# A four-layer model on one core: a new hand-written order in the gated delta attention, and three smaller moves

## Chip, core and metric

The kernel runs as one program on one core of a Trainium2 chip. A core has five engines that run side by side, each with its own instruction stream: TensorE (PE, matrix products and transposes), VectorE (DVE), ScalarE (ACT), GpSimd (POOL) and SyncE (SP), which here only issues transfers (DMA). They wait for each other by semaphores. The metric is the device time of the core in microseconds (us), less is better.

## The reference

`x` has 2 sequences of 1024 tokens with 256 channels. Four layers follow each other; in each, attention and feed-forward both read the same normalised `xn`, and both are added to the residual:

```python
xn = layernorm(x)                       # no weights
x = x + attention_l(xn) + feed_forward_l(xn)
```

- Layer 0: gated delta-rule attention with 16 heads (key and value width 128), and a feed-forward whose weights are rounded to -1, 0, 1 (width 704, sigmoid gate).
- Layer 1: causal softmax attention, 16 heads of width 128 over 4 key/value heads, output bias; feed-forward with silu gate, width 1024.
- Layer 2: rotary attention, 16 heads of width 16; 16 experts of which each token takes the best two, squared relu, weights dequantised.
- Layer 3: attention with exponential decay, 32 heads of width 64; 8 experts, best two, and a shared expert of width 704.

The delta rule of layer 0, for one head:

```python
q, k, v = silu(conv4(xn @ Wq.T)), silu(conv4(xn @ Wk.T)), silu(conv4(xn @ Wv.T))
e = k @ Wsv.T - v                       # its l2, l1 and cosine feed two small MLPs
beta, amp = sigmoid(mlp_b(stats)), mlp_a(stats)
g = -exp(A_log) * softplus(k/|k| * amp + dt_bias)     # per channel
for t in tokens:
    S = S * exp(g[t])[:, None]
    delta = (v[t] - kn[t] @ S) * beta[t]
    S = S + outer(kn[t], delta)
    o[t] = qn[t] * 128**-0.5 @ S
out += (rmsnorm(o) * norm_w * sigmoid(xn @ Wg1.T @ Wg2.T + bg2)) @ Wo.T
```

## The kernel before

**Stages.** Nine blocks follow each other: the first layer norm, the delta attention, the first feed-forward, the causal attention, the second feed-forward, the rotary attention, its experts, the decay attention, the last experts. Between two blocks all engines meet at a barrier. The residual `T.x` (tokens on partitions) and the transposed norm `T.xnT` (channels on partitions) stay in SBUF throughout. Each feed-forward normalises the residual for the next layer as its groups of 512 tokens end, the last group at its very end.

**Delta attention.** There are 64 units, one for each head and group of 512 tokens. The recurrence over tokens is turned into matrix work: chunks of 128 tokens, within a chunk a triangular system solved by doubling in seven levels (`LV` = 7, blocks of 1, 2, 4 ... 64 tokens). A new unit starts every seven slots (`SL`), and each operation X of a unit has a fixed slot `X_AT` after its start; `at(g, X_AT)` gives the unit whose X runs in slot g. So each slot holds one level of one unit, one chunk of the unit before, and parts of the preparation of two later units. Every engine has one loop over the slots, and inside it a row of `if` blocks: their order, written by hand, is the order in which that engine works. Nothing is reordered at run time, so an instruction that waits holds up all behind it on its engine.

The names that matter, by engine:

- PE: projections of k, v, q (L296, into the PSUM tensor `fr`), the values turned (L328) and their prediction, statistics `STAT` (L383), `Z` broadcasts, the diagonal `KQ` (L352), transposes of `kF` (`KH`, L376), the gate matmul (`GATE`, L323). Per level: `products(u, lv)` (L305, all pairs of tokens into `lpd`), `transposed` (L310), the x matmul (L396), the yt matmuls (L437, L439 in the last level). Level 0 has transposes of the mask instead (L451). Per chunk k (in the slots of levels 0 to 3 of the next unit): w (L341), dl (L424), o and s (L462 to L467). Then the row sums of squares with one column each (L476) and the output projection Y (L417).
- DVE: three taps of the short convolutions after the first (`convolve`, L680), the mask that copies products into the level matrices `MA` (L691), the polynomial for log(1+x) by Horner steps (L694, in parts `POLY` and `W`), `z` and `kF`, the diagonal (L752, `diag`), `R` (L770), the triangular updates `Tm` (L785, L831) and `TT` in the last level (`TT6`, L789), the halo of the convolution (L817, L819), the state `St` (L842, L844), the gated output `og` (L825).
- ACT: first taps and silu, copies of `TT` (L512), `Xs` (L569), `Dl` (L552), `y` (L560), `khat` (L549), exponentials, the tanh of the gate, squares.
- POOL: per level `scale` (L614 to L616: `kq`, `kF` and the totals of the decays), roots by power, parts of the small MLPs, the adds of `y` to the residual.

In front of the slots PE waits for all constants (6 transfers) and for memsets, computes the first gate projection g1 for all four token groups (L290; the loops issue 8 matmuls, and the trace shows each matmul call as two instructions, here 16), and waits for ACT's copies before the first unit's k projection. DVE and POOL also wait for the constants before their loops.

**Decay attention.** Steps of one unit each; after every `NU3` steps a group of 512 tokens ends with sums, a norm and the output projection. The first group's end also holds the router's logits of the last expert layer for all 16 token tiles (64 matmul instructions of nine columns, L1869), and the best two are picked in one burst of small DVE instructions (`two_best`) shortly after, at step `ROUTE + 3`.

The slots before the change:

```python
K_AT, V_AT, Q_AT, SILU_AT, VT_AT, STAT_AT, SUMS_AT, ROOT_AT = 0, 1, 2, 4, 5, 6, 7, 8
MLP_AT, MLP2_AT, HID_AT, BETA_AT, Z_AT, POLY_AT, W_AT, KQ_AT, LV_AT = 9, 10, 11, 11, 13, 14, 15, 16, 17
GATE_AT, KH_AT, CHUNK_AT, OUT_AT, RMS_AT, Y_AT = 17, 24, 24, 28, 29, 31
```

With seven slots to a unit, level 0 shares its slot with `GATE`, `KH`, the first chunk and Y of older units; level 6 shares its own with `Q_AT` and `KQ_AT`.

## Time and profile before

| | |
|---|---|
| three runs, us | 6602.77, 6605.63, 6611.05 |
| median, us | 6605.63 |
| profiled execution, us | 6588.47, of which the span is 6586.7 |
| busy share of the span | PE 92%, DVE 59%, ACT 41%, POOL 35% |
| mean granted clock of TensorE | 0.96 of full |
| instructions | 99233 |

The profile is one execution, recorded by the hardware profiler. Times in it are us from the start of the span. A line such as L305 is a line of the kernel shown above. In an order of time, a row has its start, its length, engine, line, operation, the tensors written and read, the tile, how many instructions it groups, and in brackets the idle time of the engine ahead of it with what released it. The granted clock is that which the throttle allowed TensorE: 1.0 is 2.4 GHz, 0.5 is 1.2 GHz.

### The profile page before, as it was taken

How to read it: one execution, taken by the hardware profiler on the slowest of the kernel's cores; microseconds unless marked ns; L12 is line 12 of the kernel's file. 1: busy time of each engine (PE TensorE's matmuls, PEld its weight loads, DVE VectorE, ACT ScalarE, POOL GpSimd, SP SyncE). 2: the span in 40 equal slices, each digit the busy share in tenths (PEclk: the TensorE clock that was granted, in tenths of full speed). 3: DMA queues.
4: the chain of work that ended last, by engine and by line, in shares of the span. 5: the costliest groups of instructions: out<-in, count | busy, mean ns of one | idle time of the engine just before them, and what ended most of it. 6: DMA issues, size and time to landing. Idle time of an engine off the chain costs nothing. (4 is left out here: it accounts for less than half of the span.)

```text
span 6586.7 us, 99233 instructions
## 1 busy us (share of the span) xinstructions
PE 6069.7 (92%) x37522; PEld 4392.9 (67%) x37522; DVE 3858.4 (59%) x7222; ACT 2708.2 (41%) x5584; POOL 2308.8 (35%) x2602
## 2 busy tenths in 40 slices
PE   5898989898889898988899999999999989999999
PEld 3777777777777777777477777653334667767665
DVE  5777777777777777775334444337654444444322
ACT  4445454545454444443145555413664122222211
POOL 3666667676666666675000000010000011111100
PEclk8999999999999999999999999998999999999999
DMA  0000000000000000000000000000001011211200
GB/s 29 5 5 5 3 2 5 5 5 5 5 5 1 5 5 5 5 1 1 15 18 14 12 11 12 23 7 1 1 1 52 1 62 62 68 68 68 75 7 7
DMA packets 33925, 112.56 MB, mean 17 GB/s; under 512 B 4272, under 2 KB 9648, under 8 KB 33456
## 3 DMA queue, kind: packets, MB, share of 16 engines
q1 hardware_dynamic: 33456, 106.22, 4.8%
q8 instruction: 305, 5.00, 0.3%
q14 instruction: 164, 1.34, 0.1%
HBM read 104.11 MB, written 2.10 MB: 16 GB/s over the span
## 5 line engine op out<-in xcount | busy, mean ns | idle before, releaser
L614 POOL TENSOR_TENSOR d_kq<-d_kq,d_tot 128x512 f32<-128x512 f32 x448 | 556.6, 1242 | 829.2 <-PE d_lpd L305 823.8
L305 PE MATMUL d_lpd<-d_kq,d_kF 128*128 128x128 f32 x3584 | 550.2, 302 | 110.9 <-POOL d_tot L616 103.3
L680 DVE SCALAR_TENSOR_TENSOR d_qkv<-d_raw,d_wts,d_qkv 128x512 f32<-128x512 f32 x576 | 506.8, 888 | 124.8 <-ACT d_qkv L493 120.0
L305 PEld LDWEIGHTS d_lpd<-d_kq,d_kF 128*128 128x128 f32 x3584 | 491.1, 211 | 133.1 <-POOL d_tot L616 126.5
L691 DVE COPY_PREDICATED d_MA<-d_pairs,d_lpd 128x512 f32<-128x512 int32 x384 | 316.4, 824 | 359.6 <-PE d_lpd L305 356.9
L396 PEld LDWEIGHTS d_xy<-d_Tm,d_MA 128*128 128x128 f32 x3072 | 409.4, 205 | 167.4 <-issue 165.7
L396 PE MATMUL d_xy<-d_Tm,d_MA 128*128 128x64 f32 x3072 | 434.8, 288 | 58.8 <-ACT d_TT L512 57.4
L1744 DVE TENSOR_REDUCE r_nm<-r_ps 128x2 f32<-128x1024 f32 x256 | 307.8, 1223 | 138.6 <-PE r_ps L1563 138.4
L994 POOL TENSOR_TENSOR f1rstd<-f1var,mhalf 128x4 f32<-128x4 f32 x4 | 4.0, 1009 | 1097.1 <-DVE f1var L1019 1097.1
L296 PE MATMUL d_fr<-xnT,d_wts 128*128 128x512 f32 x768 | 380.1, 618 | 0.7 <-ACT d_g1T L487 0.7
L437 PE MATMUL d_xy<-d_Xs,d_TT 128*128 128x64 f32 x2560 | 366.9, 293 | 0.2 <-ACT d_Xs L569 0.2
L1841 PE MATMUL e_pj<-xnT,e_wts 128*128 128x512 f32 x768 | 347.7, 602 | 13.5 <-DMA e_wts<-in_w3all 11.7
L437 PEld LDWEIGHTS d_xy<-d_Xs,d_TT 128*128 128x128 f32 x2560 | 358.4, 216 | 0.4 <-ACT d_Xs L569 0.4
L615 POOL TENSOR_TENSOR d_kF<-d_kF,d_tot 128x256 f32<-128x256 f32 x448 | 352.0, 786 | 0.0
L1664 ACT ACTIVATE r_pT<-r_ps 128x512 f32<-128x512 f32 x512 | 274.9, 598 | 146.3 <-PE r_ps L1571 145.7
L694 DVE SCALAR_TENSOR_TENSOR d_lp<-d_lp,d_ez 128x512 f32<-128x512 f32 x448 | 325.0, 725 | 13.1
L512 ACT ACTIVATE d_TT<-d_xy 128x256 f32<-128x256 f32 x320 | 124.5, 389 | 464.3 <-PE d_xy L310 464.3
L1304 DVE TENSOR_TENSOR c_sc<-c_sc,c_mask 128x128 f32<-128x128 f32 x256 | 76.7, 300 | 397.8 <-PE c_sc L1181 397.8
L1219 PEld LDWEIGHTS c_po<-c_pT,c_vt 128*128 128x128 f32 x2304 | 294.7, 191 | 21.0 <-ACT c_pT L1279 9.3
L1219 PE MATMUL c_po<-c_pT,c_vt 128*128 128x128 f32 x2304 | 301.9, 276 | 0.2
L1563 PE MATMUL r_ps<-r_kT,r_qT 32*128 32x512 f32 x1024 | 292.1, 694 | 2.7 <-DVE r_nm L1744 1.1
L642 POOL TENSOR_TENSOR d_pw<-d_st,d_half 128x20 f32<-128x20 f32 x64 | 257.5, 4024 | 98.6 <-DVE d_sums L706 98.5
(399 smaller groups left out, 13919.4 us busy)
## 6 DMA issues: line engine op xcount, KB each, us to landing
e_wts<-in_w3all SPq DMA_DIRECT2D x64, 897.0 KB, 4.6
d_wts<-in_headw SPq DMA_DIRECT2D x16, 583.5 KB, 3.8
c_wqo<-in_wqo SPq DMA_DIRECT2D x32, 256.0 KB, 2.6
f3ws<-in_f3w SPq DMA_DIRECT2D x17, 384.0 KB, 8.2
f2ws<-in_f2s SPq DMA_DIRECT2D x16, 256.0 KB, 6.6
f2qs<-in_f2q SPq DMA_DIRECT2D x16, 256.0 KB, 6.8
f1ws<-in_f1w SPq DMA_DIRECT2D x8, 384.0 KB, 6.4
f0ws<-in_f0w SPq DMA_DIRECT2D x6, 384.0 KB, 5.4
```

The lines of the kernel that those rows point to most:

```text
L296: last = nc.tensor.matmul(fr[:, bank, :], w_of(u)[:, w0 + kd * P:w0 + (kd + 1) * P], T.xnT[:, kd, tok(u):tok(u) + GRP], start=(kd == 0), s ...
L305: last = nc.tensor.matmul(out[:, :, k], kF[:, u % 2, ch_(k)], moving[:, :, k, :, 1], start=True, stop=True)
L396: last = nc.tensor.matmul(mh(xy[:, j * 64:(j + 1) * 64], h), MA[:, lv, ch_(j)], even(Tm[:, ch_(j)], h), start=True, stop=True)
L437: last = nc.tensor.matmul(xy[:, 256 + j * 64:256 + (j + 1) * 64], TT[:, ul % 2, ch_(j)], Xs[:, j * 64:(j + 1) * 64], start=True, stop=True)
L614: nc.gpsimd.tensor_tensor(v, v, bc(bc(t_l[:, :, 0], 2, h), 1, 2), ALU.mult)
L615: nc.gpsimd.tensor_tensor(f, f, bc(t_l[:, :, 1], 2, h), ALU.mult)
L680: step = nc.vector.scalar_tensor_tensor(qkv[:, u % 3, x], raw[:, u % 2, x, i:i + GRP], tap(u, x, i), qkv[:, u % 3, x], ALU.mult, ALU.add)
L691: nc.vector.copy_predicated(into, bc(mh(pairs[:, lv], h), 1, 2), lpd[:].rearrange("p (x m h) -> p x m h", x=2, h=h)).then_inc(masked, 1)
L694: ch.link(nc.vector.scalar_tensor_tensor(lp[:], lp[:], LOG1P[i], ez[:], ALU.add, ALU.mult))
L1219: last = nc.tensor.matmul(po[:, 0:P], vt[:, n // (4 * QT) % 2, j], pT[:, n % 2, j * P:(j + 1) * P], start=(j == 0), stop=(j == t))
L1744: nc.vector.tensor_reduce(nm[:, t % 2, half, 4 * j + i0:4 * j + i0 + 2], ps[:, row_pair(row - 1):row_pair(row - 1) + 2], AX, ALU.max).then ...
L1841: last = nc.tensor.matmul(pj[:, x % 2, :], w[:, w0 + kd * P:w0 + (kd + 1) * P], T.xnT[:, kd, g * GRP:(g + 1) * GRP], start=(kd == 0), stop ...
```

## The change

**The order in the delta attention** is written anew on all four engines.

- PE, in a slot: k projection, statistics, values, `Z`, `KQ`, w, products(0), the x matmul, Y, dl, `KH`, q projection, products, yt, o and s, the row sums, and for level 0 the transposes and products(1), then the v projection, the gate matmul, and the transposes of the later levels. `KH` moves one slot earlier (`KH_AT` 24 to 23, the slot of level 6). In the level-0 slot Y now precedes dl, o and s, and these precede the transposes and products(1); the gate goes from first to last.
- DVE: the small MLP instructions and the level-0 mask go to the front of the slot; the taps are mostly placed early; the masks precede `og`, the diagonal, `Tm` and `St`; in level 4 Horner steps precede the mask; in level 6 `TT6` and the third tap of v precede the diagonal; `kF` and the halo follow `St`.
- ACT: `khat` and `R` first, the copies of y ahead of `Dl`, then `Xs`, the squares and the evacuations of q and v, last the tanh of the gate, the error squares, `Z`, the exponential of beta and the evacuation of k.
- POOL: roots ahead of the second MLP part; scale ahead of the first `kq` product; the second scaling of level 0 behind the first two adds of y.

**The front.** The first head's weights are the first transfer, ahead of the constants. The g1 projections move to slot 3 (into the PSUM tensors `lpd`, `xy`, `ca`, `co`), with their waits for the constants and memsets; ACT copies them at the start of slot 4, ahead of its silu; PE waits for these copies at slot 17. DVE and POOL wait for the constants at slot 6.

**The norm of the first feed-forward.** It normalises three of its four groups (`norms=NG - 1`). The causal attention does the last: DVE's mean, centring and variance at its start, ACT's square between its first evacuations of keys, POOL's power ahead of the addition of the bias to the residual (which now waits for the norm), PE's eight transposes after the first two score tiles, ACT's two copies into `T.xnT` after the first softmax tile.

**The routing.** The logits come in three portions, at the ends of the first three groups: 8, 4 and 4 token tiles. `ROUTE` goes from `NU3 + 1` to `3 * NU3 + 1`, and `two_best` is cut into four parts that run at steps `ROUTE + 3` to `ROUTE + 6`; the shared gate follows at `ROUTE + 7`.

The core of the diff (the moves within ACT, POOL and DVE are given by some of their lines; "..." stands for lines left out):

```diff
-GATE_AT, KH_AT, CHUNK_AT, OUT_AT, RMS_AT, Y_AT = 17, 24, 24, 28, 29, 31
+GATE_AT, KH_AT, CHUNK_AT, OUT_AT, RMS_AT, Y_AT = 17, 23, 24, 28, 29, 31
...
+        G1_SLOT = 3
...
+                sp.dma_start(wts[:, 0], ins["headw"][0]).then_inc(loaded[0], 16)
...
-                pe.wait_ge(const_loaded, 96)
-                pe.wait_ge(consts_set, 4)
-                for t in range(NG):
-                    for kd in range(KD):
-                        last = nc.tensor.matmul(fr[:, t, :], wg1[:, kd], T.xnT[:, kd, t * GRP:(t + 1) * GRP], start=(kd == 0), stop=(kd == KD - 1))
-                    last.then_inc(g1_mm, 1)
-                pe.wait_ge(g1_copied, NG)
...
+                    if g == G1_SLOT:
+                        pe.wait_ge(const_loaded, 96)
+                        pe.wait_ge(consts_set, 4)
+                        for t, bank in enumerate((lpd, xy, ca, co)):
+                            for kd in range(KD):
+                                last = nc.tensor.matmul(bank[:], wg1[:, kd], T.xnT[:, kd, t * GRP:(t + 1) * GRP], start=(kd == 0), stop=(kd == KD - 1))
+                            last.then_inc(g1_mm, 1)
+                    if g == LV_AT:
+                        pe.wait_ge(g1_copied, NG)
...
+                    if level and lv == 0:
+                        pe.wait_ge(kq0_ready, ul + 1)
+                        pe.wait_ge(kq1_ready, ul + 1)
+                        if ul:
+                            pe.wait_ge(masked, 7 * ul)
+                        products(ul, 0)
...
+                    if level and lv == 0:
+                        pe.wait_ge(mask0_ready, ul + 1)
+                        for j in range(NC):
+                            last = nc.tensor.transpose(xy[:, ch_(j)], MA[:, 0, ch_(j)], T.ident[:])
+                        last.then_inc(tr_mm, 1)
+                        pe.wait_ge(scaled, 7 * ul + 1)
+                        pe.wait_ge(masked, 7 * ul + 1)
+                        products(ul, 1)
...
+                    if g == G1_SLOT + 1:
+                        for t, bank in enumerate((lpd, xy, ca, co)):
+                            act.wait_ge(g1_mm, t + 1)
+                            nc.scalar.activation(g1T[:, t * GRP:(t + 1) * GRP], bank[:], ACT.Copy).then_inc(g1_copied, 1)
...
+                    if g == STAT_AT:
+                        dve.wait_ge(const_loaded, 96)
...
+                    if (u := at(g, Z_AT)) is not None:
+                        nc.vector.tensor_tensor(kF[:, u % 2], qkv[:, u % 3, 1], fr[:, 2, :], ALU.mult).then_inc(kF_ready, 1)
                     if (u := at(g, Q_AT + 1)) is not None:
                         dve.wait_ge(conv[0], u + 1)
...
-def feed_forward(nc, T, name, NTL, kind, w, weigh=None, blocks=None, prepare=None, raw=None, ternary=False, out=None):
+def feed_forward(nc, T, name, NTL, kind, w, weigh=None, blocks=None, prepare=None, raw=None, ternary=False, out=None, norms=NG):
...
-                if out is None:
+                if out is None and norms == NG:
                     turn(NG - 1)
...
+                pe.wait_ge(xn_ready, 1)
+                for kd, into in enumerate((po, py)):
+                    for j in range(NC):
+                        last = nc.tensor.transpose(into[:, j * P:(j + 1) * P], xn[:, j, kd * P:(kd + 1) * P], T.ident[:])
+                    last.then_inc(turned, 1)
...
                 pool.wait_ge(consts, 32)
+                pool.wait_ge(xn_ready, 1)
                 nc.gpsimd.tensor_tensor(T.x[:], T.x[:], bc(bias[:], 1, NT), ALU.add).then_inc(biased, 1)
...
-        ROUTE = NU3 + 1
+        ROUTE = 3 * NU3 + 1
+        tiles_at = {0: (0, 8), 1: (8, 12), 2: (12, 16)}
...
-                            if gu == 0:
+                            if gu in tiles_at:
                                 pe.wait_ge(gate_loaded, 32)
-                                for t in range(NT):
+                                for t in range(*tiles_at[gu]):
...
-                        two_best(nc, ch, E3, p, e1, key, sel, both, top, tot, order, T.w3, 0)
+                    if ROUTE + 3 <= n < ROUTE + 7:
+                        two_best(nc, ch, E3, p, e1, key, sel, both, top, tot, order, T.w3, 0, parts=(n - ROUTE - 3,))
+                    if n == ROUTE + 7:
...
-    feed_forward(nc, T, "f0", 6, "sigmoid", ins["f0w"], prepare=quantise, ternary=True)
+    feed_forward(nc, T, "f0", 6, "sigmoid", ins["f0w"], prepare=quantise, ternary=True, norms=NG - 1)
```

## Rows read from the trace of the kernel before

**Rows 1.** The page: busy us, share of the span and instructions of each engine.

```profile
PE 6069.7 (92%) x37522; PEld 4392.9 (67%) x37522; DVE 3858.4 (59%) x7222; ACT 2708.2 (41%) x5584; POOL 2308.8 (35%) x2602
```

**Rows 2.** Busy us by stretch (PE, PEld, DVE, ACT, POOL), then granted clock, DMA share, GB/s.

```profile
46.50:3141.90 3095.40, 2740.85 (x18432) 2246.26 (x18432) 2334.07 (x4446) 1465.95 (x2961) 2074.60 (x2384) 0.94 0.01 4
...
1010.14:1055.48 45.34, 40.45 (x292) 32.85 (x291) 37.08 (x72) 22.92 (x47) 31.80 (x37) 1.00 0.05 14
```

**Rows 3.** Line L439: shortest/median/longest ns, first and last start (us), tile, count.

```profile
L439 PE MATMUL d_xy<-d_TT,d_Xs x512: 222/222/367, 154.2 to 3117.9; 128*64 128x64 f32 x171
```

**Rows 4.** PE's waits, 1000 to 2900 us: total us, how often, longest.

```profile
PE d_lpd L305 <- POOL d_tot L616: 67.3, 40, 2.6
```

**Rows 5.** PE in order of time, one unit at full clock.

```profile
1010.14 0.68 PE L439 MATMUL d_xy<-d_TT,d_Xs 128*64 128x64 f32 x8
...
1011.93 0.60 PE L376 MATMUL d_fr<-ident,d_kF 128*128 128x128 f32 x4
...
1017.77 1.18 PE L305 MATMUL d_lpd<-d_kq,d_kF 128*128 128x128 f32 x8 [1.37 <-POOL d_tot L616]
...
1021.47 0.49 PE L341 MATMUL d_ca<-d_St,d_kq 128*128 128x128 f32 x2 [1.85 <-DVE d_St L844]
...
1045.21 0.66 PE L310 MATMUL d_xy<-ident,d_Tm 128*128 128x128 f32 x4 [0.66 <-DVE d_Tm L831]
```

**Rows 6.** DVE in order of time, the same unit.

```profile
1011.31 0.69 DVE L752 TENSOR_TENSOR d_MA<-d_fr,ident 128x512 f32<-128x512 f32 x1
...
1019.21 1.30 DVE L691 COPY_PREDICATED d_MA<-d_pairs,d_lpd 128x512 f32<-128x512 int32 x1
1020.31 0.85 DVE L817 COPY d_raw<-d_raw 128x9 f32<-128x9 f32 x1
...
1042.55 0.73 DVE L691 COPY_PREDICATED d_MA<-d_pairs,d_lpd 128x512 f32<-128x512 int32 x1 [1.38 <-PE d_lpd L305]
...
1043.76 0.94 DVE L694 SCALAR_TENSOR_TENSOR d_lp<-d_lp,d_ez 128x512 f32<-128x512 f32 x1
```

**Rows 7.** Line L680, the convolution's taps on DVE: as in the third group.

```profile
L680 DVE SCALAR_TENSOR_TENSOR d_qkv<-d_raw,d_wts,d_qkv x576: 725/750/1976, 49.9 to 3004.5; 128x512 f32<-128x512 f32 x192
```

**Rows 8.** ACT and POOL in order of time, the same unit.

```profile
1016.01 0.28 ACT L552 ACTIVATE d_Dl<-d_ca 128x128 f32<-128x128 f32 x1 [2.85 <-PE d_ca L424]
1016.18 1.56 ACT L560 ACTIVATE d_y<-d_fr,d_rr 128x256 f32<-128x256 f32 x4
...
1013.59 2.31 POOL L614 TENSOR_TENSOR d_kq<-d_kq,d_tot 128x512 f32<-128x512 f32 x1 [0.92 <-PE d_lpd L305]
...
1017.11 0.61 POOL L616 TENSOR_TENSOR d_tot<-d_tot 128x256 f32<-128x256 f32 x1
```

**Rows 9.** SP, PE and ACT in order of time, the front of the delta attention.

```profile
28.46 0.34 SPq L272 DMA_DIRECT2D d_wsv<-in_wsvT  x1
...
36.07 9.83 PE L290 MATMUL d_fr<-xnT,d_wg 128*128 128x512 f32 x16 [9.00 <-DMA d_pairs<-in_pairs]
...
56.73 1.48 ACT L523 ACTIVATE d_qkv<-d_qkv 128x1536 f32<-128x1536 f32 x1 [0.89 <-DVE d_qkv L680]
```

**Rows 10.** The page's transfers: count, KB each, median us from issue to landing.

```profile
d_wts<-in_headw SPq DMA_DIRECT2D x16, 583.5 KB, 3.8
```

**Rows 11.** End of the first feed-forward and start of the causal attention, order of time.

```profile
3285.97 1.29 DVE L1004 TENSOR_TENSOR x_res<-f0py,x_res 128x512 f32<-128x512 f32 x2 [4.74 <-PE f0py L903]
...
3298.39 0.33 SPq L1128 DMA_DIRECT2D c_wkv<-in_wkv  x1
...
3303.48 8.85 POOL L1294 TENSOR_TENSOR x_res<-x_res,c_bias 128x4096 f32<-128x4096 f32 x1 [9.87 <-DMA c_bias<-in_bo]
```

**Rows 12.** Two group ends of the decay attention by stretch, and the router's line.

```profile
5521.09:5549.84 28.75, 27.18 (x168) 23.11 (x169) 6.90 (x16) 3.23 (x6) 2.59 (x2) 0.76 0.10 33
5754.41:5771.35 16.94, 15.77 (x100) 11.73 (x101) 6.66 (x14) 3.35 (x7) 2.59 (x2) 0.90 0.17 55
...
L1869 PE MATMUL e_md<-e_gw,xnT x64: 257/362/362, 5530.7 to 5541.5; 128*128 128x9 f32 x64
```

More of the change, by code:

```diff
@@ new lines, in _ @@
+                    if chunk:
+                        dve.wait_ge(s_mm, 4 * uc + k + 1)
+                        if first(uc) and k == 0:
+                            nc.vector.tensor_copy(St[:, uc % 2], ca[:, 0:P]).then_inc(s_ready, 1)
+                        else:
+                            nc.vector.scalar_tensor_tensor(St[:, uc % 2], St[:, uc % 2], tot[:, uc % 2, tot_at[LV] + k:tot_at[LV] + k + 1],
+                                                           ca[:, 0:P], ALU.mult, ALU.add).then_inc(s_ready, 1)
@@ L984, in _ @@
                         spread(g - 1)
-                if out is None:
+                if out is None and norms == NG:
                     square(NG - 1)
@@ L991, in _ @@
                 if out is None:
-                    for g in range(NG):
+                    for g in range(norms):
                         pool.wait_ge(var_ready, g + 1)
@@ L1067, in _ @@
                 add(NG - 1)
-                if out is None:
+                if out is None and norms == NG:
                     centre(NG - 1)
@@ L1269, in _ @@
                 probs(0)
+                for kd, into in enumerate((po, py)):
+                    act.wait_ge(turned, kd + 1)
+                    nc.scalar.activation(T.xnT[:, kd, LAST], into[:], ACT.Copy).then_inc(copied, 1)
                 for n in range(STEPS):
@@ L1330, in _, with two_best, pick @@
                 add(STEPS - 1)
-def two_best(nc, ch, E, p, rest, key, sel, both, top, tot, order, weights, floor):
+def two_best(nc, ch, E, p, rest, key, sel, both, top, tot, order, weights, floor, parts=(0, 1, 2, 3)):
     TTS = lambda o, a, b, op: ch.link(nc.vector.tensor_tensor(o, a, b, op))
-    ch.link(nc.vector.tensor_reduce(tot[:], p[:], AX, ALU.add))
-    ch.link(nc.vector.reciprocal(tot[:], tot[:]))
-    TTS(p[:], p[:], bc(tot[:], 2, E), ALU.mult)
-    ch.link(nc.vector.tensor_copy(rest[:], p[:]))
-    for best in range(2):
+    def pick():
         ch.link(nc.vector.tensor_reduce(top[:], rest[:], AX, ALU.max))
```

446 lines of the change are left out of this document (225 added, 221 removed).

## The prediction

> **What bounds the kernel now.** I read the page, then the busy time by stretch, then PE's waits, then the order of time where the diff touches. One execution spans 6586.7 us and TensorE (PE) is busy for 92% of it [rows 1], so only time in which PE stands still, or runs at its lower clock, can come back. The delta attention is 3095.4 us of it, with PE busy for 2740.9 us at a granted clock of 0.94 [rows 2]. Its 64 units (one head and 512 tokens each) are one pipeline: the last-level matmul L439 starts at 154.2 us in the first and at 3117.9 us in the last [rows 3], so a unit takes 2963.7 / 63 = 47.0 us. A unit at full clock took 45.34 us, of which PE was busy 40.45 [rows 2]. A unit thus loses some 4.8 us to waits and 47.0 - 45.3 = 1.7 us to the clock.
>
> The waits are short and return in each unit: over 1900 us PE waited 40 times for POOL's L616, 67.3 us in all [rows 4]. In the full-clock unit the waits are 1.37 us for that (level 0), 1.85 us for the state St (start of level 1) and 0.66 us for Tm (end of level 4) [rows 5]. DVE is the second bound: in the level-0 slot a mask of 1.30 us and the halo copy of 0.85 us stand between products(1) and St [rows 6], and nothing PE has left covers them.
>
> **The delta order, slot by slot.** I walk one unit at full clock; t = 0 is the start of L439 (1010.14), and the St wait ends at 1021.47, t = 11.33 [rows 5].
>
> Levels 3 and 4. kF, a product of the shape that takes 0.69 us [rows 6], moves behind St, and the last of POLY's Horner steps (0.94 us beside other work [rows 6], taken as 0.7 alone) moves ahead of the mask. DVE was idle for 1.38 us before that mask [rows 6], which just holds both (0.69 + 0.7); so both are hidden there, and the Tm update no longer queues behind the Horner step. PE's 0.66 us goes: **-0.6**. Without that cover it stays. The statistics now go first in level 3 and wait for ACT's error squares, just in time by my walk: **+0.1**.
>
> Level 5. The third tap of k (median 0.75 us [rows 7]) moves ahead of the last mask, so Tm is 0.75 later, less the 0.6 won. PE has the V projection to do meanwhile, and the next x matmul waits for an ACT copy that itself queues behind V's evacuation: **+0.1**; with nothing to cover it, +0.75.
>
> Levels 6 and 0. The transposes of kF (0.60 us by the record, about 0.43 by what they hold up [rows 5]) move from level 0 to level 6: no change for PE. On DVE the last subtraction (TT6, about 0.4 us) now stands ahead of the third tap of v (0.75) and of the diagonal product (0.69), and TT6 waits for L439. So the diagonal ends at 0.6 + 0.1 + 0.4 + 0.75 + 0.7 = 2.6 us at the earliest, and the output projection Y waits for it. PE is ready for Y after L439 (0.6), one state matmul (0.2) and products(0) (1.0), at 1.8: a **new wait of about 0.8 us**. Y, with twice the columns of products(0), takes some 1.8 (to 4.4), and ACT now copies y (1.56 us) before Dl (0.28 [rows 8]), so that the state matmuls start at 4.4 + 0.1 + 1.56 + 0.28 + 0.1 = 6.4; they now stand ahead of the transposes. State 0.5, transposes 0.44 and products(1) 1.0 end at 8.3. POOL's three scalings, 1013.59 to 1017.72 or 4.1 us [rows 8], end at 6.0 to 6.6 and are no longer last: the 1.37 us wait goes. The gate matmul (1.0) follows products(1), under DVE's mask (1.30), which ends at 9.7; St, now ahead of the halo copy, ends at 10.0, and with contention I take 10.35. Against 11.33 that is -1.0, of which 0.43 was paid in level 6: **-0.55**.
>
> Level 1. The halo copy (0.85 us [rows 6]; a memset in every second unit) now stands between St and R. R, and the matmul that needs it, are later by up to 0.85, and what follows on DVE (rounding, mask, Tm) with it: **+0.7**, or 0 if the copy finds POOL silent.
>
> At full clock: -0.6 + 0.1 + 0.1 - 0.55 + 0.7 = -0.25; I take **-0.2 us a unit**. Bounds: the cover in level 5 missed (0.65) and one more wait behind POOL of 0.6 make +1.0; level 1's loss at 0 makes -1.0. Queued behind Y's new wait are the chunk, products(1) and the gate on PE, ACT's y copies, and behind them POOL's adds, which have slack.
>
> The clock. Its price is 1.7 us a unit. Ahead of its falls PE either stood for 1.37 and 1.85 us around products(1), or did one-column matmuls and then stood for 0.66 us [rows 5]. Now level 0 has waits of 0.8, 0.8, 0.5 and 1.0 us with dense matmuls between, and the 0.66 is gone. I give back half, between nothing and all: **-0.85**. Over 63 units: -63 x 1.05 = **-66 us**, between 63 x 1.0 = +63 and -63 x 2.7 = -170.
>
> The port. A tap L680, with both inputs in SBUF, takes 0.75 us by the median and 1.98 at most [rows 7], while the diagonal, fed from PSUM, keeps its 0.69. The Trainium skill, "SBUF — State Buffer", section "SBUF: two separate sides", says that DVE and GpSimd share a pair of ports by an exclusive lock that the holder keeps for a whole instruction. The trace agrees in size: the excess of 1.2 us is one POOL instruction of rows 8. By that rule, which speaks against this order, a tap that is placed among the scalings pays one more instruction, and the result is rival 3's.
>
> **The front.** Before, PE starts the g1 projections at 36.07, when the last constant has landed, and the first unit's silu starts at 56.73 [rows 9]. Now the first head's weights are the first DMA, at 28.5 [rows 9], and such a transfer takes 3.8 us in the median [rows 10], so K starts near 32.4. Q is done near 40, and the 16 g1 matmuls (9.83 us in the row, in part at half clock; some 7 by estimate) end near 47. ACT copies them ahead of the silu, which starts near 48.7. **-8 us**, between -5 (g1 held by the constants, now one transfer later) and -14 (g1 fully hidden).
>
> **The norm of the first feed-forward.** The last adds end at 3287.3 and the next stage's first DMA goes out at 3298.39 [rows 11]; without the norm it goes some 0.9 us after the adds: -10.3. In the attention the norm's DVE and ACT work lies before the first scores, where DVE has nothing to do; its transposes stand where PE waits for the first softmax; two copies of 0.6 us push ACT's first turned tile by some 0.5. POOL's bias add (8.85 us [rows 11]) starts at +12 instead of +5 us and ends at +21, when DVE wants it: +0.3. **-9.5 us**, between -7 and -10.5 (were the transposes not covered, 2 us).
>
> **The routing.** The group end with all logits took 28.75 us at a clock of 0.76, one without took 16.94 at 0.90 [rows 12]. The 64 nine-column matmuls (median 362 ns, minimum 257 [rows 12]) are shared out as 32, 16 and 16. They took 0.175 us apiece, mostly at half clock; at full clock I estimate 0.11, so 7 to 9.2 us for 11.2, plus 0.6 for copies at two more group ends, less 0.6 for the routing chain that is split over four steps. **-3 us**, between 0 and -4.5.
>
> **The sum.** -66 - 8 - 9.5 - 3 = -86.5. From the profiled execution's 6588.5 us (its span and 1.8 around it) that is 6502; the median of the three runs, 6605.6, lies 17 us above it, and from there I predict **6519 us**.
>
> **The rivals.** (1) As above, 6519, by itself 6470 to 6570: 0.50. (2) The order does more: both large waits go and nothing replaces them, -63 x (1.6 + 0.85) = -154, with the edges' -20.5: 6431. For it: those two waits are the largest; against: Y's new wait. 0.17. (3) Slower: the chain TT6, tap, diagonal, Y, y, Dl is lengthened by DVE waiting out POOL instructions. At +1.0 us a unit and no relief of the clock it is +63 - 20.5: 6648. It decides from +0.33 us a unit, which eats the edges. For it: DVE is full there; against: one mask wait is now off the path. 0.13. (4) The order changes nothing, each wait is replaced by another and the clock falls as often: 6605.6 - 20.5 = 6585. For it: my walk gives only -0.2. 0.20, of which 0.08 is within 13 us of now.
>
> **The numbers.** 0.2% (13 us) is about what a measurement of this kernel can tell from no change. Faster: 0.49 + 0.17 + 0.12 = 0.78; same: 0.01 + 0.08 = 0.09; slower 0.13. The range runs from rival 2 to the edge of no change, 6430 to 6610, and leaves out rival 3 and the far end of the bounds.
>
> **What would show it.** L439 to L439 falls from 47.0 to 46.0 us; the stage's clock rises from 0.94 towards 0.97; PE's wait for L616 goes and a wait of Y for the diagonal appears near 0.8 us; the wait for Tm shrinks; R comes later after St. The first silu starts near 48.7, the attention's first DMA goes out right after the adds, and the first group end of the decay attention takes some 23 us. I am wrong if Y's wait is well over 1 us, or if the clock stays at 0.94.

## The result, and the profile after

The changed kernel takes 6397.5 us (median of four runs, 6394.5 to 6400.1); the kernel before takes 6607.3 beside it. The ratio is 0.968 (95% interval 0.967 to 0.970): 210 us faster, where 86.5 were predicted, and below the range.

In the profiled executions it is 6588.5 against 6397.0 us, 191.5 less. The other 18 us are the distance of the kernel before from its own profiled execution, which was faster than every other execution of it on record (the fastest took 6593.7); the changed kernel has no such distance (6397.0 and 6397.5).

Where they went can be read from three starts. First the page and the stretch of the delta attention after (columns as in [rows 1] and [rows 2]), with one unit at full clock:

```profile
PE 5965.5 (93%) x37522; PEld 4271.9 (67%) x37522; DVE 3804.0 (59%) x7226; ACT 2694.1 (42%) x5584; POOL 2288.9 (36%) x2602
...
46.50:2957.50 2911.00, 2632.43 (x18423) 2124.68 (x18421) 2273.63 (x4436) 1450.10 (x2955) 2054.70 (x2384) 0.98 0.01 4
1034.57:1078.54 43.97, 39.62 (x287) 32.21 (x286) 36.42 (x70) 22.67 (x46) 31.84 (x37) 1.00 0.00 1
```

The last-level matmul, now L436, and the router's line, now L1913 (shortest/median/longest ns, first and last start in us):

```profile
L436 PE MATMUL d_xy<-d_TT,d_Xs x512: 222/222/366, 147.6 to 2933.8; 128*64 128x64 f32 x171
L1913 PE MATMUL e_md<-e_gw,xnT x64: 257/257/363, 5339.6 to 5790.9; 128*128 128x9 f32 x64
```

- The first unit's L436 starts at 147.6 instead of 154.2: the front is worth 6.6 us.
- From there the last unit's start is 2786.2 us away instead of 2963.7 [rows 3]: 177.5 us, a unit of 44.2 instead of 47.0 us.
- From that to the first DMA of the causal attention it is 3103.64 - 2933.8 = 169.8 instead of 180.5 us [rows 3, 11]: 10.7 us for the norm.
- The rest of the program takes 2.9 us longer; the rotary attention, whose code is the same, takes 3.3 longer. The decay attention with the routing (first matmul to the next stage's first) took 903.5 us before and 902.7 after. Neither difference can be told from the scatter: in the traces of all 17 kernels of this study the rotary attention takes 600.6 to 607.9 us, and the decay attention 901.0 to 905.4 with the old routing and 898.7 to 905.5 with the new.

So the order of the delta attention is what has to be explained. PE in order of time, the unit of the window above; t = 0 is 1034.57:

```profile
1034.57 0.68 PE L436 MATMUL d_xy<-d_TT,d_Xs 128*64 128x64 f32 x8
...
1037.61 1.99 PE L401 MATMUL d_fr<-d_wo,d_og 128*128 128x256 f32 x8 [1.12 <-DVE d_MA L825]
1039.44 0.38 PE L408 MATMUL d_ca<-d_R,d_TT 128*128 128x128 f32 x2
1041.52 0.46 PE L449 MATMUL d_ca<-d_Dl,d_khat 128*128 128x128 f32 x2 [1.70 <-ACT d_Dl L552]
...
1045.07 0.49 PE L372 MATMUL d_ca<-d_St,d_kq 128*128 128x128 f32 x2 [0.67 <-DVE d_St L833]
1045.40 1.00 PE L389 MATMUL d_xy<-d_Tm,d_MA 128*128 128x64 f32 x8
1046.35 0.49 PE L408 MATMUL d_ca<-d_R,d_TT 128*128 128x128 f32 x2
...
1067.04 1.00 PE L459 MATMUL d_fr<-ones,d_osq 128*128 128x1 f32 x8
1067.91 0.63 PE L304 MATMUL d_xy<-ident,d_Tm 128*128 128x128 f32 x4
1069.11 1.08 PE L389 MATMUL d_xy<-d_Tm,d_MA 128*128 128x64 f32 x8 [0.56 <-ACT d_TT L517]
...
1073.98 0.66 PE L304 MATMUL d_xy<-ident,d_Tm 128*128 128x128 f32 x4 [0.24 <-DVE d_Tm L829]
```

The reader is to see four things. Y (L401) waits 1.12 us for the diagonal (predicted 0.8); the state matmul L449 waits 1.70 us for Dl behind ACT's copies of y (predicted to start at t = 6.4, it is 6.95); the St wait ends at t = 10.50 (predicted 10.35, before 11.33). And in level 4 the transposes L304 follow the one-column matmuls L459 with no wait, where they stood for 0.66 us [rows 5].

The three largest of PE's waits, 1000 to 2800 us (total us, times, longest). All eight groups come to 144 us there; before, five groups made up 191 us of 1900 (the largest is [rows 4]):

```profile
PE d_ca L449 <- ACT d_Dl L552: 49.1, 40, 1.7
PE d_xy L389 <- ACT d_TT L517: 26.2, 51, 0.6
PE d_ca L372 <- DVE d_St L835: 17.1, 21, 1.2
```

The two units at full clock differ by 45.34 - 43.97 = 1.4 us. The units on average differ by 2.8. The other half is the clock. The trace records the stretches in which TensorE was granted 1.2 GHz; summed from first to last unit and divided by 63 they are 5.15 us a unit before and 1.64 after. I call this the half-clock time below. Of the first 60 units, 14 have none of it before, at 45.13 us on average, and 39 after, at 43.89.

### The profile page after: what moved, and what is told of

Same layout as the page of the kernel before. It is cut to its first block and busy times, and to the rows that moved or that the text cites. A ratio compares the mean times of both kernels' runs of the same rounds, so it can differ in the third digit from the quotient of the medians.

```text
span 6394.8 us, 99261 instructions
## 1 busy us (share of the span) xinstructions
PE 5965.5 (93%) x37522; PEld 4271.9 (67%) x37522; DVE 3804.0 (59%) x7226; ACT 2694.1 (42%) x5584; POOL 2288.9 (36%) x2602
## 5 line engine op out<-in xcount | busy, mean ns | idle before, releaser
L683 DVE SCALAR_TENSOR_TENSOR d_qkv<-d_raw,d_wts,d_qkv 128x512 f32<-128x512 f32 x576 | 531.9, 924 | 43.1 <-ACT d_qkv L492 35.6
L299 PE MATMUL d_lpd<-d_kq,d_kF 128*128 128x128 f32 x3584 | 520.5, 290 | 33.9 <-POOL d_kq L646 27.2
L299 PEld LDWEIGHTS d_lpd<-d_kq,d_kF 128*128 128x128 f32 x3584 | 458.9, 199 | 58.0 <-POOL d_kq L646 26.7
L389 PEld LDWEIGHTS d_xy<-d_Tm,d_MA 128*128 128x128 f32 x3072 | 388.6, 196 | 92.3 <-issue 90.8
L389 PE MATMUL d_xy<-d_Tm,d_MA 128*128 128x64 f32 x3072 | 406.1, 276 | 43.9 <-ACT d_TT L517 43.9
L434 PE MATMUL d_xy<-d_Xs,d_TT 128*128 128x64 f32 x2560 | 329.5, 273 | 0.0
L697 DVE SCALAR_TENSOR_TENSOR d_lp<-d_lp,d_ez 128x512 f32<-128x512 f32 x448 | 310.9, 694 | 13.2
L434 PEld LDWEIGHTS d_xy<-d_Xs,d_TT 128*128 128x128 f32 x2560 | 318.6, 196 | 0.0
L1193 PE MATMUL c_sc<-c_kT,c_qT 128*128 128x512 f32 (+3 forms) x768 | 290.2, 487 | 0.7 <-ACT c_qT L1264 0.7
L1614 PE MATMUL r_ps<-r_qT,r_kT 32*128 32x512 f32 x1024 | 279.5, 652 | 0.8 <-ACT r_pT L1707 0.8
```

The costliest lines, as they stand in the source:

```text
L299: last = nc.tensor.matmul(out[:, :, k], kF[:, u % 2, ch_(k)], moving[:, :, k, :, 1], start=True, stop=True)
L389: last = nc.tensor.matmul(mh(xy[:, j * 64:(j + 1) * 64], h), MA[:, lv, ch_(j)], even(Tm[:, ch_(j)], h), start=True, stop=True)
L434: last = nc.tensor.matmul(xy[:, 256 + j * 64:256 + (j + 1) * 64], TT[:, ul % 2, ch_(j)], Xs[:, j * 64:(j + 1) * 64], start=True, stop=True)
L683: step = nc.vector.scalar_tensor_tensor(qkv[:, u % 3, x], raw[:, u % 2, x, i:i + GRP], tap(u, x, i), qkv[:, u % 3, x], ALU.mult, ALU.add)
L697: ch.link(nc.vector.scalar_tensor_tensor(lp[:], lp[:], LOG1P[i], ez[:], ALU.add, ALU.mult))
```

## The experiments

First the numbers, so that each text can be short. "Before" is the kernel before on the same chip; the columns from "unit" on are read from the one profiled execution of each kernel; a unit is (last start - first start) / 63; "full" is the mean of those of the first 60 units that have no half clock; the two last columns count the starts of half-clock stretches in all 63 units, those in the 20 us behind L439 or L436 (levels 0 to 2) and those later in the unit (nearly all at the end of level 4 or in level 5).

```
kernel              us      before   ratio (95%)              unit   full   half-clock  early late
before            6607.3                                     47.03  45.13  5.15        21    49
changed           6397.5   6607.3   0.968 (0.967 to 0.970)   44.21  43.89  1.64         8    19
order_only        6413.4   6611.5   0.969 (0.968 to 0.971)   44.22  43.85  1.59         4    21
edges_only        6585.5   6611.5   0.996 (0.995 to 0.997)   47.12  45.24  5.33        24    46
halo_first        6397.7   6611.5   0.967 (0.966 to 0.968)   44.22  44.10  1.37         8    13
before_filler     6508.6   6611.5   0.984 (0.983 to 0.985)   45.76  45.56  1.68        27     1
after_filler      6365.5   6605.8   0.964 (0.963 to 0.965)   43.80  43.95  0.27         1     2
horner_late       6544.5   6605.8   0.991 (0.990 to 0.993)   46.55  44.66  5.06         1    54
level0_old        6412.3   6605.8   0.971 (0.970 to 0.972)   44.56  44.22  1.92        22     4
v2                6408.9   6605.8   0.971 (0.969 to 0.972)   44.27  43.90  1.79         9    19
before_horner     6466.1   6608.2   0.978 (0.977 to 0.980)   44.98  44.81  1.74        29     2
horner_late_filler 6424.7  6608.2   0.972 (0.970 to 0.973)   44.62  44.82  0.49         6     0
v3                6520.6   6608.2   0.986 (0.985 to 0.988)   46.16  45.28  2.30        37     3
v4                6517.1   6608.2   0.986 (0.984 to 0.988)   45.93  45.18  2.03        32     3
before_filler4    6557.7   6611.9   0.992 (0.990 to 0.993)   46.60  45.45  3.68        45     1
before_filler0    6613.9   6611.9   1.000 (1.000 to 1.001)   47.37  none   6.50         1    63
after_filler_split 6396.4  6611.9   0.967 (0.966 to 0.969)   44.21  43.83  1.53         0    25
```

**order_only and edges_only.** The change cut in two: the kernel before with the new order alone, and with front, norm and routing alone.

> The kernel before with only the new delta order on the four engines (KH_AT included); front, norm of the first feed-forward and routing as before. Theory A, from the two traces: the order carries the result; the units take 44.2 us instead of 47.0, which is 63 x 2.8 = 177 us in the profiled executions, and the median of before lies some 18 us above its profiled one, so 6607 - 177 - 18 = 6412, between 6405 and 6435. Rival B, the term as predicted (-1.05 us a unit): 6541. Rival C, the order needs the front's other start to fall into its phase: anything from 6450 up, with units above 45 us.

> The kernel before with the new front, the moved norm and the routing in portions, and the old delta order. Theory A: the three are worth what the traces show between the stages' first matmuls, 6.7 + 10.5 + 0.9 = 18 us: 6589, with units of 47 us. Rival C, they also shift the delta units or the later stages: a distance over 8 us from 6589. The prediction had 20.5 us: 6587.

The order alone has the units of the changed kernel, 44.22 us; the edges alone leave them at 47.1 and give 26 us (0.996, 19 to 36 us) by the medians. The 18 us that the trace of the changed kernel shows at these three places lie just below that interval, and order_only is 16 us above the changed kernel, so the two parts add up to the whole within some 15 us.

**halo_first.** The changed kernel with the halo copy where it was on DVE, which tests the prediction's loss in level 1.

```diff
+                    if (u := at(g, Q_AT + 1)) is not None:
+                        dve.wait_ge(conv[0], u + 1)
...
                     if chunk:
                         dve.wait_ge(s_mm, 4 * uc + k + 1)
```

> The changed kernel with the halo copy (or memset) of the convolution back in front of the state update St on DVE, in every unit. Theory A: in the changed order the gap between St and R is PE's round trip through the w matmul (about 0.7 us), and the halo copy lies in it at no cost; put back in front of St it delays St by its 0.5 us (the copy, every second unit) or 0.1 us (the memset): +0.3 us a unit, with a fall of the clock now and then, 6410 to 6440. Rival B, the prediction's term: behind St the copy delays R by up to 0.85 us, so putting it back gains 0.3 to 0.7 us a unit: 6353 to 6378. Rival C: DVE has slack at both places, 6397 within 8.

The time is the same (6397.7). The units are not quite: those at full clock with the copy (every second unit; the others have a memset) take 44.29 us instead of 43.97, as theory A said, yet the units on average take 44.22 as before, with less half-clock time (1.37 against 1.64). At full clock the copy is thus a little better off behind St, and the prediction's +0.7 is not there; theory A's loss of time did not come. DVE and then PE in the changed kernel, around St, in a unit with the copy, show why:

```profile
1088.43 0.32 DVE L833 COPY d_St<-d_ca 128x128 f32<-128x128 f32 x1
1088.67 0.50 DVE L843 COPY d_raw<-d_raw 128x9 f32<-128x9 f32 x1
1089.08 0.41 DVE L736 SCALAR_TENSOR_TENSOR d_hid<-d_hid,d_mlp 128x256 f32<-128x256 f32 x1
1089.53 0.35 DVE L759 SCALAR_TENSOR_TENSOR d_R<-d_vtok,d_pw,d_ca 128x128 f32<-128x128 f32 x1
```

```profile
1088.81 0.49 PE L372 MATMUL d_ca<-d_St,d_kq 128*128 128x128 f32 x2 [0.67 <-DVE d_St L833]
1089.14 1.00 PE L389 MATMUL d_xy<-d_Tm,d_MA 128*128 128x64 f32 x8
1089.98 0.44 PE L408 MATMUL d_ca<-d_R,d_TT 128*128 128x128 f32 x2
```

Between St and R lies PE's w matmul (L372, started at 1088.81, 0.49 us long), so R cannot start before about 1089.3 whatever DVE does, and what DVE does in that gap costs little. Behind w, PE has the x matmul (1.00 us) ahead of the matmul that needs R (L408), which started without a wait.

**before_filler.** The kernel before with more work: matmuls that nobody reads (fillers), in PE's waits. The first of the three below stands three times in a row.

```diff
+                    if level and lv == 1:
+                        pe.wait_ge(tm0_ready, ul + 1)
+                        nc.tensor.matmul(xy[:, 256:512], T.ident[:], T.xnT[:, 0, 0:256], start=True, stop=True)
...
+                    if level and lv == 4:
+                        pe.wait_ge(masked, 7 * ul + 6)
+                        nc.tensor.matmul(lpd[:, 0:256], T.ident[:], T.xnT[:, 0, 0:256], start=True, stop=True)
                     if level and 1 <= lv < 6:
                         pe.wait_ge(tm_ready, 5 * ul + lv)
                         transposed(ul)
+                    if level and lv == 4:
+                        nc.tensor.matmul(lpd[:, 0:256], T.ident[:], T.xnT[:, 0, 0:256], start=True, stop=True)
```

> The kernel before with added matmuls whose results nobody reads, placed in PE's waits: three of 256 columns ahead of the wait for St (level 1), one of 256 ahead of the wait for Tm and one behind the transposes of level 4; nothing else differs. It does more work. Theory A: a good part of the gain of the change is the clock (half-clock time fell from 5.15 to 1.3 us a unit), and the clock falls because PE stands still or does one-column matmuls there; with the waits filled the half-clock time goes below 3 us a unit and the units fall from 47.0 to between 45.2 and 46.3 us: 6495 to 6565. Rival D, the clock falls for another reason: the fillers cost nothing or some tenths each, 6607 to 6630, with half-clock time above 4.5 us a unit.

103 us faster by adding work. A unit at full clock is 0.43 us longer than before, and yet the mean unit is 1.27 us shorter: the half-clock time fell from 5.15 to 1.68 us. So the clock, and not only the waits, was worth over 100 us in the kernel before.

**horner_late and level0_old.** Two parts of the order undone, each alone: on DVE the Horner step of level 4 goes back behind the gated output and ahead of Tm; on PE the gate goes first in level 0, and its transposes and products(1) ahead of the chunk.

```diff
-                    if (u := at(g, POLY_AT)) is not None:
-                        horner(u, 3)
...
                         nc.vector.scalar_tensor_tensor(og[:], tg[:, u % 2], 1.0, co[:], ALU.add, ALU.mult).then_inc(og_ready, 1)
+                    if (u := at(g, POLY_AT)) is not None:
+                        horner(u, 3)
```

> The changed kernel with one Horner step of level 4 put back behind the mask and the gated output, as before, so that it stands ahead of the Tm update. Theory A, the prediction's step: the wait for Tm in level 4 comes back with 0.6 us a unit, 38 us, and with it some of the clock: 6425 to 6460. Rival: the one-column matmuls and other work on PE cover it now: 6397 within 8.

> The changed kernel with PE's part of level 0 as before: the gate matmul first, and the transposes and products(1) ahead of the chunk's o and s; DVE, ACT and POOL keep the new order. Theory A: in level 0 DVE is the bound (no gap on it from 0.5 us before L436 to the St update at 10.4 us), so PE's own order matters little: 6397 within 15, units of 44.0 to 44.5 us. Rival B, the prediction's walk: products(1) waits for POOL's scaling again (1 us or more) and St comes behind it, +0.6 to +1.0 us a unit, with more half clock: 6440 to 6500.

The one Horner step, 0.7 us of DVE's work a unit, costs 147 us in 6397. PE's moves in level 0, undone, cost 15 us: the wait for POOL's scaling is back (63.5 us in 30 waits over 1800 us), but the one for Dl is gone. Level 4 with the step put back, PE in order of time, and then two windows of the same unit, up to the waits and behind them (columns as in [rows 2]):

```profile
1114.20 1.00 PE L459 MATMUL d_fr<-ones,d_osq 128*128 128x1 f32 x8
1115.87 0.66 PE L304 MATMUL d_xy<-ident,d_Tm 128*128 128x128 f32 x4 [0.66 <-DVE d_Tm L829]
1117.09 1.94 PE L389 MATMUL d_xy<-d_Tm,d_MA 128*128 128x64 f32 x8 [0.56 <-ACT d_TT L517]
```

```profile
1082.25:1116.25 34.00, 30.25 (x230) 25.57 (x230) 26.36 (x52) 19.48 (x39) 21.77 (x27) 1.00 0.00 1
1116.95:1123.75 6.80, 6.66 (x26) 5.96 (x27) 5.64 (x13) 0.38 (x1) 6.55 (x7) 0.50 0.00 0
```

One-column matmuls, 0.66 us of wait, short transposes, 0.56 us of wait: then the clock is at 1.2 GHz for 6.8 us, and the x matmul takes 1.94 instead of 1.08 us. Such stretches start in the later part of the unit, nearly all in this place, 54 times in 63 units. In the changed kernel the first of the two waits is absent, and 19 stretches start there.

**after_filler.** The changed kernel with three such matmuls in the wait for Dl and one in the wait for TT.

> The changed kernel with added matmuls whose results nobody reads in two of PE's waits: three of 256 columns between dl and the wait for Dl in level 0, one between the transposes of level 4 and the x matmul of level 5. Theory A: the half-clock time that is left (1.6 us a unit, at a price of 0.3) falls below 0.8, and the time by 5 to 20 us: 6377 to 6392. Rival D: what is left of the half clock has other causes, or the added matmuls are late themselves as they cost 0.4 us a unit at full clock in the kernel before: 6395 to 6425.

All of the first 60 units are now at full clock, and it is 6365.5 us, some 32 us under the changed kernel, beyond both intervals and more than the 5 to 20 us expected. The mean unit fell by 0.41 us, 26 us in all; the rest lies behind the units, where 4 us of it are the scatter of the decay attention. The unit at full clock has not changed (43.95 and 43.89): the filler costs nothing in these two waits. This is the fastest version of the study; the share of each of the two places was not run.

**v2.** Level 0 once more, by the finding that DVE has no gap there.

On PE the transposes of level 0 and the gate go between dl and the wait for Dl, and TT of level 0 is awaited at yt, not at x. On DVE St goes ahead of mask(1), TT of level 0 behind it, and hid3 (a step of the small MLP) and the halo behind R.

> The changed kernel with level 0 rearranged once more: on PE the level-0 transposes and the gate matmul stand in the wait for Dl, and TT of level 0 is awaited at the yt matmul, not at x; on DVE St stands ahead of mask(1), TT of level 0 behind the mask, and the halo and hid3 behind R. Theory A (DVE is the bound of level 0, 0.7 to 1.0 us of TT0 leaves its chain, and PE has no gate left behind products(1)): -0.5 to -0.8 us a unit, 6345 to 6370. Rival: the mask is late anyway (POOL's scaling holds it for 1.3 us instead of 0.7) or R is late behind TT0: 6385 to 6410.

6408.9 us, full units of 43.90 as before: the rival was right. The wait for Dl went (8 us of waits in 1800 us instead of 49), and over the full-clock units the x matmul of level 1 starts 0.6 us earlier; level 1 then takes 0.6 us longer. In the place of the wait for Dl came one for the mask (48.4 us in 41 waits), because the mask of level 0 is 1.31 us long beside POOL's scaling, which starts with it. DVE and POOL:

```profile
1054.42 1.31 DVE L696 COPY_PREDICATED d_MA<-d_pairs,d_lpd 128x512 f32<-128x512 int32 x1 [0.94 <-PE d_lpd L299]
```

```profile
1054.49 1.29 POOL L618 TENSOR_TENSOR d_kq<-d_kq,d_tot 128x512 f32<-128x512 f32 x1
```

**before_horner and horner_late_filler.** The Horner step alone, moved in the kernel before; and the changed kernel without that step, but with matmuls in the two waits.

```diff
+                    if (u := at(g, POLY_AT)) is not None:
+                        horner(u, 3)
                     if level and lv < 6:
                         mask(ul, lv + 1)
...
-                    if (u := at(g, POLY_AT)) is not None:
-                        horner(u, 3)
```

> The kernel before with a single move: in level 4 one Horner step on DVE goes ahead of the mask, where DVE was idle for 1.38 us, instead of behind the gated output and ahead of the Tm update. Theory A, from the run that put it back in the changed kernel (147 us): this one step is the larger part of the gain also by itself, as the 0.66 us wait for Tm, right behind the one-column matmuls, is what most falls of the clock follow (48 of 70 in the kernel before); 0.6 us of wait and about 1.2 us of clock a unit, 6480 to 6515, half-clock time 1.5 to 2.5 us a unit. Rival E: the other half of the falls (behind level 0's waits) then comes in the freed place, as the halo, tap and gate order is still the old one: only the wait goes, 6555 to 6580.

> The changed kernel with the Horner step put back ahead of the Tm update, and in the waits that this makes on PE two matmuls of 256 columns that nobody reads, one ahead of the transposes of level 4 and one behind them. Theory A splits the 147 us of the run without them in 0.77 us a unit of wait (49 us) and the rest, 98 us, of clock; the added matmuls give the clock back and not the wait: 6440 to 6465, half-clock time below 2 us a unit. Rival F: the clock falls because of the longer unit or of DVE's later work: 6530 to 6550, half-clock time near 5 us.

The single move gives 142 us, two thirds of the whole change. Level 4 in that kernel, first PE, then DVE:

```profile
1090.54 1.00 PE L476 MATMUL d_fr<-ones,d_osq 128*128 128x1 f32 x8
1091.40 0.64 PE L310 MATMUL d_xy<-ident,d_Tm 128*128 128x128 f32 x4
1092.60 1.07 PE L396 MATMUL d_xy<-d_Tm,d_MA 128*128 128x64 f32 x8 [0.56 <-ACT d_TT L512]
```

```profile
1086.01 2.87 DVE L694 SCALAR_TENSOR_TENSOR d_lp<-d_lp,d_ez 128x512 f32<-128x512 f32 x4
1089.53 0.74 DVE L691 COPY_PREDICATED d_MA<-d_pairs,d_lpd 128x512 f32<-128x512 int32 x1 [0.65 <-PE d_lpd L305]
1090.16 0.67 DVE L827 SCALAR_TENSOR_TENSOR d_og<-d_tg,d_co 128x512 f32<-128x512 f32 x1
1090.75 0.41 DVE L831 TENSOR_TENSOR d_Tm<-d_Tm,d_xy 128x256 f32<-128x256 f32 x1
```

Four Horner steps stand ahead of the mask, and 0.65 of the 1.38 us that DVE idled there [rows 6] is left. The full unit fell by 0.32 us, the mean unit by 2.05; so nearly all is the clock. With the step late and the waits filled, the unit at full clock stays long (44.82) but the half-clock time is 0.49 us: of horner_late's 147 us, 120 came back with the Horner step left where it was.

**v3 and v4.** v2 with products released before POOL's totals, and with fillers, two in the wait for the level-1 mask and one in that for TT behind level 4; v4 has the one-column matmuls split around the transposes instead of this last one.

```diff
-                        pe.wait_ge(scaled, 7 * ul + 1)
+                        pe.wait_ge(kf_scaled, 7 * ul + 1)       # incremented one POOL instruction earlier
```

> The rearranged level 0 of the earlier run (6409 us) with two additions: products wait for the scaling of kq and kF only and no longer for the totals (a semaphore of its own, about 1.06 us earlier in level 0 and 0.4 in level 1), and added matmuls that nobody reads, two of 256 columns in the wait for mask(1) and one in that for TT of level 5. Theory A: 0.3 to 0.6 us a unit of wait go and the half-clock time falls below 0.5 us a unit: 6335 to 6365. Rival G: the mask of level 0 stays 1.3 us long beside POOL's scaling and follows products(1) wherever that is, and DVE's own chain takes the rest: 6370 to 6390.

> As the run before it in this set, but instead of the added matmul in the wait for TT of level 5 the one-column matmuls of the row sums are split, two ahead of the transposes of level 4 and two behind them, and DVE's RMS step follows one Horner step later. Theory A: 0.3 us less a unit than that run, as the wait for TT is filled with work that has to be done: 6315 to 6345. Rival: with only one-column matmuls in that place the clock falls there again: half-clock time above 1.5 us a unit and 6350 to 6390.

Both are slower by 108 to 112 us than v2, which neither text expected. The products do come earlier, and so does POOL's next scaling in level 1. DVE and POOL there in v3, and DVE's same instruction in v2:

```profile
1088.57 0.42 DVE L821 TENSOR_SCALAR d_qkv<-d_qkv 128x512 f32<-128x512 f32 x1
1088.91 1.37 DVE L823 TENSOR_SCALAR d_qkv<-d_qkv 128x512 f32<-128x512 f32 x1
1090.20 0.88 DVE L827 TENSOR_SCALAR d_qkv<-d_qkv 128x512 f32<-128x512 f32 x1
```

```profile
1088.82 1.18 POOL L625 TENSOR_TENSOR d_kq<-d_kq,d_tot 128x512 f32<-128x512 f32 x1 [0.75 <-PE d_lpd L299]
1089.96 0.84 POOL L626 TENSOR_TENSOR d_kF<-d_kF,d_tot 128x256 f32<-128x256 f32 x1
```

```profile
1058.31 0.42 DVE L816 TENSOR_SCALAR d_qkv<-d_qkv 128x512 f32<-128x512 f32 x1
```

```profile
1092.07 1.10 PE L304 MATMUL d_xy<-ident,d_Tm 128*128 128x128 f32 x4 [1.77 <-DVE d_Tm L849]
```

Of 0.42 us the rounding (L823) became 1.37, beside POOL's scaling that began 0.1 us before it, and the next one 0.88 beside POOL's second; the mask and Tm behind them are late, and PE waits 1.77 us for Tm in level 1, a place that had no such wait. The three roundings of a unit take 2.68 us together in v3 and in v4, in every unit, and 1.26 in v2; the full-clock unit is 1.38 us longer in v3 than in v2 (45.28 against 43.90). And most stretches at half clock now start behind this wait: 37 and 32 early ones instead of 9. It is the mechanism of the prediction's third rival, VectorE waiting out GpSimd, at another place than the one named there, brought in by an edit that released POOL too early. The Trainium skill ("SBUF — State Buffer", section "SBUF: two separate sides") says that VectorE, in a mode that uses both ports or with two SBUF inputs, and GpSimd lock a shared pair of ports for whole instructions; by that rule the rounding waits out what is left of POOL's instruction. The trace agrees in size: 1.09 us were left (1088.91 to 1090.00), and the excess is 0.95 us. Which mode the rounding ran in no run here shows. The fillers are not likely to have a part: the one for TT is absent in v4, whose full-clock unit is 45.18 us; the two for the mask were not left out in any run.

**before_filler4, before_filler0 and after_filler_split.** The filler of the kernel before, in one place each; and after_filler with the wait for TT filled by half of the one-column matmuls instead.

> The kernel before with only the two added matmuls of level 4 (256 columns each, ahead of the transposes and behind them), none in level 0. Theory A: the falls that follow the one-column matmuls and the waits for Tm and TT (48 of 70, 245 of 330 us of half clock) go, those behind level 0 stay: half-clock time 1.5 to 2.5 us a unit, 6500 to 6530. Rival H: both places share one budget, and what is filled at one comes out at the other: above 6560, with the falls moved to level 0.

> The kernel before with only the three added matmuls ahead of the wait for St in level 0, none in level 4. Theory A: at most the falls of level 0 go (21 of 70, 82 us of half clock, worth some 30 us), and in the run with both places 27 falls were there nonetheless: 6580 to 6625, half-clock time above 4 us a unit. Rival H, the shared budget, or level 0 as the cause of those at level 4 too: below 6550.

> The changed kernel with the three added matmuls in level 0's wait for Dl, as in after_filler, but in level 4 instead of an added matmul the one-column row sums split, two ahead of the transposes and two behind them, and DVE's RMS step one Horner step later. Theory A: the wait for TT is filled with work that has to be done, 0.3 us less a unit than after_filler's 6365 at the same clock: 6340 to 6355. Rival I: the one-column matmuls do not hold the clock where a full one does: half-clock time above 1 us a unit, 6360 to 6390.

Level 4 alone gives 54 us and level 0 alone nothing; both together gave 103. The falls move: with level 4 filled the late ones go (49 to 1) and the early ones rise from 21 to 45; with level 0 filled the early ones go and every unit has a late one. Each theory had one of the two runs: the shared budget had the falls of before_filler4 right (and its time but for 2 us), theory A those of before_filler0. The places are not independent, and not one budget either. In level 4 the kind of matmul makes a difference: after_filler_split has 25 late falls with half of the one-column matmuls in the wait for TT, where after_filler has 2 with two instructions of 256 columns there (the split also moves one small DVE step). PE still waits for TT for up to 0.3 us in the split and not at all in after_filler; but before_filler4 keeps such waits, of up to 0.3 us, beside its 256-column matmuls and has 1 late fall. It is no rule for all places, though: v4 has the same split and 3 late falls, beside 32 early ones.

## Why the prediction was wrong

It had the direction, the places and nearly every wait; it had the size wrong by more than half, in two steps.

- **The clock** is the step that failed: "I give back half, between nothing and all: -0.85". The price of the half clock was 47.03 - 45.13 = 1.90 us a unit and is 44.21 - 43.89 = 0.32 now: -1.58 us, or 100 us where 54 were put down. (edges_only, with the old order too, has 1.88.) The prediction spread the loss over all waits ahead of the falls. The runs show one place above all: the wait for Tm behind the one-column matmuls of level 4, which the step "levels 3 and 4" itself removed. It priced that step at its 0.6 us; undone it costs 2.3 us a unit, done alone it gives 2.05.
- **Level 1** is the second step that failed, "+0.7, or 0 if the copy finds POOL silent": it was 0, and not for that reason. The gap between St and R is PE's w matmul, and the copy lies in it. A step that moves behind a handshake with another engine has the round trip as cover.

The other terms can be set beside the full-clock units (mean of 14 before and 39 after). "Level 0" is L439 or L436 to the x matmul of level 1; level n is that x matmul to the next, level 6 the last one to L439 or L436.

```
level      0      1      2      3      4      5      6     unit
before   11.30   5.79   7.19   5.85   5.94   6.27   2.78   45.13
after    10.68   5.78   7.12   5.75   5.13   6.26   3.17   43.89
```

- **Levels 3 and 4**, -0.6 and +0.1: -0.9, nearly all in level 4. **Level 5**, +0.1: 0. **Levels 6 and 0**, -0.55: -0.62 in level 0 and +0.39 for the transposes of kF in level 6, -0.23 (-0.43 in the two units shown). The new wait of Y is 1.12 where 0.8 was said.
- In sum -0.25 was walked for a full-clock unit and -1.24 measured. Of the difference of 1.0, level 1 is 0.7, levels 3 and 4 are 0.4, levels 2 and 5 are 0.2, and levels 6 and 0 gave 0.3 less than said.
- **The front** -8: 6.6. **The norm** -9.5: 10.7. **The routing** -3: 0.8, which the scatter of that stage hides; the nine-column matmuls are mostly at full clock now (median 257 instead of 362 ns [rows 12]), yet the stage is hardly shorter; where the rest went was not tried.
- Rival 2, "both large waits go and nothing replaces them", -154 us, had a chance of 0.17 and the nearest time, for a reason that did not hold: the waits were replaced (Y and Dl, 2.8 us together). What went was the clock's loss. For rival 3 the excess of 1.2 us was set beside "one POOL instruction of rows 8"; those show 2.31 and 0.61 us, and the one that fits is L615 between them (1.29 us). The 17 us between profile and median were taken as common to both kernels; they belong to the one before.

That most late falls hang on the wait for Tm is shown: they went from 49 to 2 when it was removed and from 19 to 54 when it was put back. Filled together with the wait for TT it leaves 1 (before_filler4) or none (horner_late_filler). Most of the 19 that the changed kernel keeps start at the x matmul right behind the wait for TT; with a 256-column filler there, and those in the wait for Dl, they are 2. What the one-column matmuls ahead of these waits do is only argued: they were never moved away as a whole. Why level 0's falls rise as level 4's go is open.

## What to carry to other kernels

Where the granted clock is below one, look which wait stands just ahead of each fall, and price that wait by the clock it costs as well as by its length; here 0.66 us was worth 2 us. Before reordering anything, fill the suspected waits with matmuls that nobody reads, all of them in one run: it tells what the clock is worth at least, and the fillers may be kept. One wait at a time misleads: alone the two places gave 54 us and nothing, together 103, and removing the one wait gave 142. When an instruction is released earlier on GpSimd, check what VectorE is doing at its new place.

## What had not been expected of the hardware

- More work made the kernel before 103 us faster and the changed one 32 us faster.
- Eight one-column matmul instructions keep PE busy for 1.00 us by the record; half of them in the wait for TT left 25 late falls of the clock, a 256-column matmul in that wait 2.
- A filler in one wait moved the falls: with level 4 filled the early ones rose from 21 to 45, with level 0 filled the late ones from 49 to 63.
- A DVE instruction of 0.42 us took 1.37 us beside a POOL instruction of 1.18 us.
